# Cross-attention on one Trainium2 core: projection pieces on four 32-column tiles, issued behind PV

## The reference

```python
q = _split_heads(hidden_states @ w_q, HEADS)
k = _split_heads(text @ w_k, HEADS)
v = _split_heads(text @ w_v, HEADS)
out_text = _merge_heads(_sdpa(q, k, v))              # softmax(q k^T / 4) v
out_ip = _merge_heads(_sdpa(q, k_ip, v_ip, mask=mask_ip))
out = (out_text + IP_SCALE * out_ip) @ w_out + b_out + residual
```

## Time and profile before

| | |
|---|---|
| median of 3 runs | 2136.64 us (2120.46 to 2138.08) |
| profiled execution | 2130.14 us, span of the records 2128.3 us |
| TensorE matmul busy | 2011.5 us, 95% of the span |
| VectorE busy | 1341.9 us, 63% |
| ScalarE busy | 1231.1 us, 58% |
| GpSimd busy | 275.6 us, 13% |
| mean granted TensorE clock | 0.978 of full speed |

### The profile page before, as it was taken

The page is one execution under the profiler, slowest core; times in us unless marked ns, Lnnn a source line. Parts: engine busy times, 40 slices in busy tenths (PEclk is TensorE's granted clock), DMA queues, the critical chain, the costliest instruction groups (busy, mean ns, idle before and its releaser), DMA issues.

```text
span 2128.3 us, 31016 instructions
## 1 busy us (share of the span) xinstructions
PE 2011.5 (95%) x12048; PEld 824.6 (39%) x12048; DVE 1341.9 (63%) x1623; ACT 1231.1 (58%) x2364; POOL 275.6 (13%) x314
## 2 busy tenths in 40 slices
PE   4899999997999999999999999999999999999987
PEld 2443334432344333443334433444334443344332
DVE  4757666565665676666755667656766567666660
ACT  0256566555565566555655566655666556665665
POOL 3001111101111011111111111011110111111100
PEclk8999899999999999999999999999999999999999
DMA  7234433353333544435333353333533344443301
GB/s 196 53 53 84 112 67 74 74 117 75 63 76 71 129 81 76 76 66 144 68 70 72 68 141 61 73 61 73 134 66 76 64 119 90 83 77 67 74 21 41
DMA packets 94309, 174.86 MB, mean 82 GB/s; under 512 B 37937, under 2 KB 62386, under 8 KB 90322
## 3 DMA queue, kind: packets, MB, share of 16 engines
q1 hardware_dynamic: 86066, 144.55, 35.1%
q10 hardware_dynamic: 7936, 28.18, 3.9%
q0 software_dynamic: 160, 0.14, 0.1%
HBM read 117.75 MB, written 48.82 MB: 78 GB/s over the span
## 4 chain that ended last, share of the span: by engine, by line
PE 84%; DMA 4%; issue 4%; ACT 4%; DVE 2%; ACTq 1%; SPq 1%; POOL 0%; POOLq 0%
PE pv_bank L580 22%; PE exp_bank L566 19%; PE max_bank L548 14%; PE work_bank L474 10%; PE work_bank L445 10%; PE work_bank L489 3%; PE work_bank L455 3%; DMA q_stack<-neg_rows 3%; ACT probs L754 2%; DVE quarter_max L853 1%; PE work_bank L467 1%; ACT probs_tail L754 1%; ACTq L738 1%; ACTq L763 1%; DMA ctxt<-in_ctx_t 0%
## 5 line engine op out<-in xcount | busy, mean ns | idle before, releaser
L853 DVE TENSOR_REDUCE quarter_max<-max_bank 128x2 f32<-128x800 f32 x1280 | 1232.4, 989 | 692.0 <-PE max_bank L548 687.7
L754 ACT ACTIVATE probs<-exp_bank 128x512 f32<-128x512 f32 x1872 | 1016.2, 595 | 528.3 <-PE exp_bank L566 501.0
L548 PE MATMUL max_bank<-k_stack,q_stack 48*128 48x400 f32 x2560 | 542.7, 384 | 55.9 <-issue 28.2
L566 PE MATMUL exp_bank<-q_stack,k_stack 50*128 50x512 f32 x1872 | 507.3, 469 | 19.9 <-ACT probs L754 19.7
L580 PE MATMUL pv_bank<-probs,v_ones 128*17 128x512 f32 x3840 | 512.5, 606 | 2.0 <-ACT probs L754 2.0
L566 PEld LDWEIGHTS exp_bank<-q_stack,k_stack 50*128 50x128 f32 x1872 | 227.9, 186 | 501.6 <-ACT probs L754 473.5
L548 PEld LDWEIGHTS max_bank<-k_stack,q_stack 48*128 48x128 f32 x2560 | 271.8, 189 | 244.7 <-issue 105.5
L445 PE MATMUL work_bank<-ctxt,wk 128*64 128x400 f32 x1280 | 257.8, 523 | 12.9 <-DMA ctxt<-in_ctx_t 11.1
L474 PE MATMUL work_bank<-wv,ctxt 128*128 128x320 f32 x768 | 246.1, 455 | 0.4 <-ACT neg_rows L698 0.4
L996 POOL TENSOR_TENSOR k_parts<-k_full,zero 128x400 fp32r<-128x400 f32 x80 | 68.2, 852 | 930.4 <-ACT k_full L698 930.4
L474 PEld LDWEIGHTS work_bank<-wv,ctxt 128*128 128x128 f32 x768 | 136.3, 191 | 85.5 <-issue 39.9
(11 more groups left out here) (86 smaller groups left out, 585.4 us busy)
## 6 DMA issues: line engine op xcount, KB each, us to landing
k_stack<-scratch_k SPq DMA_DIRECT2D x240, 200.0 KB, 6.1
scratch_k<-k_parts SPq DMA_DIRECT2D x80, 400.0 KB, 4.7
ctxt<-in_ctx_t ACTq DMA_DIRECT2D x28, 800.0 KB, 9.1
q_stack<-scratch_q SPq DMA_DIRECT2D x240, 64.0 KB, 2.3
scratch_q<-q_parts SPq DMA_DIRECT2D x80, 128.0 KB, 6.7
r_wide<-scratch_r SPq DMA_DIRECT2D x40, 256.0 KB
o_t<-o_sum SPq DMA_DIRECT2D x160, 32.0 KB, 2.0
xres<-in_x SPq DMA_DIRECT2D x8, 640.0 KB, 4.3
```

Source lines behind the costliest of these rows:

```text
L548: last = nc.tensor.matmul(max_bank[:, (u % 2) * 2 + side, 0:CHUNK], exact(q_stack[stack, slot, c, t * 128:(t + 1) * 128]), exact(k_stack[s ...
L566: nc.tensor.matmul(bank[:, :], exact(k_stack[stack, slot, c, kt * 128:(kt + 1) * 128]), exact(q_stack[stack, slot, c, :]), start=True, sto ...
L754: nc.scalar.activation(dst, exp_place(n, final), ACT.Exp, scale=SCALE).then_inc(probs_ready, 1)
L853: nc.vector.reduce_max(quarter_max[:, :, u // QUARTERS, u % QUARTERS], max_bank[:, (u % 2) * 2:(u % 2) * 2 + 2, 0:CHUNK], AX.X).then_inc(m ...
```

## The change

Each projection matmul of K, Q, V, OUT and IP is cut along its output partitions into strips of 32 (`strips`), so that it becomes up to four matmuls with 32 weight columns each, on the four 32-column tiles that PV uses. The moving operand is the same and is read by each strip. K and Q, which were two 64-column matmuls, become four of 32. Q's third contraction tile now has 128 rows instead of 64; the missing rows of `wq` and `xt` are set to zero once (two VectorE memsets, and the waits on `cleared` count two more). WA, WB, TA and TB keep their form. Then, in TensorE's program, `work` moves from the end of the step to directly behind `pv_tile`, ahead of exponent tiles 2 and 3 and of the last units. No other engine's order changes.

```diff
+            def strips(rows):
+                return [(at, min(32, rows - at)) for at in range(0, rows, 32)]
...
-                        last = nc.tensor.matmul(work_bank[half * GR:(half + 1) * GR, 0:CHUNK],
-                                                wk[:, ct, (g % NG) * GR:(g % NG + 1) * GR], ctxt[:, ct, keys:keys + CHUNK],
-                                                start=(ct == 0), stop=(ct == CT - 1))
+                        for at, rows in strips(GR):
+                            dims = (g % NG) * GR + at
+                            last = nc.tensor.matmul(work_bank[half * GR + at:half * GR + at + rows, 0:CHUNK],
+                                                    wk[:, ct, dims:dims + rows], ctxt[:, ct, keys:keys + CHUNK],
+                                                    start=(ct == 0), stop=(ct == CT - 1))
...
-                        last = nc.tensor.matmul(work_bank[:, 0:D], ctxt[:, ct, t * 128:(t + 1) * 128], wv[:, ct, :],
-                                                start=(ct == 0), stop=(ct == CT - 1))
+                        for at, rows in strips(128):
+                            key = t * 128 + at
+                            last = nc.tensor.matmul(work_bank[at:at + rows, 0:D], ctxt[:, ct, key:key + rows], wv[:, ct, :],
+                                                    start=(ct == 0), stop=(ct == CT - 1))
...
                             pv_tile(group_no - 1, (g - 1) % NG, FULL)
+                        if (g, kt) in plan:
+                            work(b, *plan[g, kt], first, last)
                         if kt < FULL:
                             exp_tile(group_no, kt, 2)
                             exp_tile(group_no, kt, 3)
                         next_units(places[2])
-                        if (g, kt) in plan:
-                            work(b, *plan[g, kt], first, last)
...
             nc.vector.memset(zero[:, :], 0.0).then_inc(cleared, 1)
+            nc.vector.memset(wq[64:128, 2, :], 0.0).then_inc(cleared, 1)
+            nc.vector.memset(xt[64:128, 2, :], 0.0).then_inc(cleared, 1)
```

More of the change, by code:

```diff
@@ L452, in q_piece @@
                 for ct in ct_range:
-                    rows = (128, 128, 64)[ct]
                     for half in range(2):
[L455 to L458, removed]
+                        for at, rows in strips(GR):
+                            dims = (g % NG) * GR + at
+                            last = nc.tensor.matmul(work_bank[half * GR + at:half * GR + at + rows, 0:QHALF],
+                                                    wq[:, ct, dims:dims + rows], xt[:, ct, half * QHALF:(half + 1) * QHALF],
+                                                    start=(ct == 0), stop=(ct == 2))
                 if ct_range[-1] == 2:
@@ L466, in ip_piece @@
                 for n in range(2):
-                    last = nc.tensor.matmul(work_bank[:, n * 64:(n + 1) * 64], q_full[:, n * 128:(n + 1) * 128],
-                                            kip_own[:, g % NG, :, :].rearrange("p h t -> p (h t)"), start=True, stop=True)
+                    for at, rows in strips(128):
+                        last = nc.tensor.matmul(work_bank[at:at + rows, n * 64:(n + 1) * 64],
+                                                q_full[:, n * 128 + at:n * 128 + at + rows],
+                                                kip_own[:, g % NG, :, :].rearrange("p h t -> p (h t)"), start=True, stop=True)
                 last.then_inc(work_full, 1)
             def v_piece(t, ct_range):
-                if t < FULL:
-                    for ct in ct_range:
-                        last = nc.tensor.matmul(work_bank[:, 0:D], ctxt[:, ct, t * 128:(t + 1) * 128], wv[:, ct, :],
-                                                start=(ct == 0), stop=(ct == CT - 1))
-                else:
-                    for ct in ct_range:
-                        for odd in range(2):
-                            last = nc.tensor.matmul(work_bank[odd * TAIL:odd * TAIL + TAILV, 0:D],
-                                                    ctxt[:, ct, FULL * 128:TEXT], wv[:, ct, :],
-                                                    start=(ct == 0), stop=(ct == CT - 1))
+                for ct in ct_range:
+                    if t < FULL:
+                        for at, rows in strips(128):
+                            key = t * 128 + at
+                            last = nc.tensor.matmul(work_bank[at:at + rows, 0:D], ctxt[:, ct, key:key + rows], wv[:, ct, :],
+                                                    start=(ct == 0), stop=(ct == CT - 1))
+                    else:
+                        for odd in range(2):
+                            for at, rows in strips(TAILV):
+                                key = FULL * 128 + at
+                                last = nc.tensor.matmul(work_bank[odd * TAIL + at:odd * TAIL + at + rows, 0:D],
+                                                        ctxt[:, ct, key:key + rows], wv[:, ct, :],
+                                                        start=(ct == 0), stop=(ct == CT - 1))
                 if ct_range[-1] == CT - 1:
@@ L487, in out_piece @@
                 for k in k_range:
-                    rows = (128, 128, 97, 128)[k]
-                    last = nc.tensor.matmul(bank, o_t[0:rows, k, t * 128:(t + 1) * 128], wout[0:rows, k, :],
-                                            start=(k == 0), stop=(k == k_end))
+                    deep = (128, 128, 97, 128)[k]
+                    for at, rows in strips(128):
+                        last = nc.tensor.matmul(bank[at:at + rows, :], o_t[0:deep, k, t * 128 + at:t * 128 + at + rows],
+                                                wout[0:deep, k, :], start=(k == 0), stop=(k == k_end))
                 if k_range[-1] == k_end:
@@ L615, in _ @@
                     pe.wait_ge(x_loaded, 32)
+                    pe.wait_ge(cleared, 3)
                     q_piece(piece[1], share(3, turn))
@@ L627, in _ @@
                 else:
-                    pe.wait_ge(cleared, 7)
+                    pe.wait_ge(cleared, 9)
                     negative_piece(0)
@@ L781, in _ @@
                     copy(vip[0:64, 2, :], work_bank[0:64, 128:192]).then_inc(work_empty, 1)
-                    act.wait_ge(cleared, 7)
+                    act.wait_ge(cleared, 9)
                 elif piece[0] == "V":
```

## The result

| | before | changed |
|---|---|---|
| median | 2135.72 us (2120.46 to 2138.08, 4 runs) | 2357.49 us (2341.85 to 2359.82, 4 runs) |
| ratio | | 1.104, 95% interval 1.097 to 1.111 |
| profiled execution | 2130.14 us | 2359.51 us |
| mean granted clock | 0.978 | 0.975 |

The change makes the kernel 10.4% slower. The forecast was 2382 us, 1% above what was measured, in a range of 2320 to 2465.

What follows compares the result with a forecast made beforehand. The prediction took ScalarE's 1.67 us wait, open in every step, as the bound: each step 3.26 us plus W. Net 262 - 6 - 20 - 1 = +235, plus 10 for the clock, gave 2375 profiled, 2382 median, range 2320 to 2465.

Steps and rivals of the forecast that it cites:

- The floor of 3.26 us: Step without a piece: PV 0.98, ScalarE's wait 1.67, tile 1 to PV 0.61; light pieces hide under it.
- W: Streaming time of a piece behind PV: whole V or OUT 2.15 us, halves 1.08, K 1.34 or 0.67, IP 0.4.
- the faster rival: All steps: form changes vanish and nothing waits, near 0.4 us saved a step, about 1955 us; chance 0.03.
- The sum: Over 441 steps, new less old length by kind of piece: 262 us more, net +235 after savings elsewhere.
- the small four: Four small pieces, unchanged in form, priced between nothing and one K tile (0.67): 37 x 0.4 = 15 us.
- 26 saved: At kt = 12, 6 us saved on the switch; at group starts, about 20 of roughly 30 us stack-load waits gone.
- the 6 for the switch: At kt = 12 the order stays and only the change of form goes: 39 x 0.15 = 6 us saved.
- 10 for the clock: Over the whole kernel, 10 us added to the net +235 for TensorE's clock.
- No further cost: Steps with three units: the last waits for VectorE until 1.77 us behind tile 2's load, when tile 1's weights are in.
- The switches go and nothing waits: All steps: a V step takes 4.33 us against 4.70, 176 us saved in all, about 1955 us; chance 0.03.
- Strips don't run together: Pieces: strips reading the same moving data cost 1.3 passes, adding 130 us (2510), or far more one after another; chance 0.03.
- The clock rival: TensorE idles about 0.7 us a step, so its clock falls more often, adding 130 to 150 us, about 2520; chance 0.05.

Runs made afterwards that it cites:

- short exponents: Exponent tiles on ScalarE cut to 64 of 512 columns behind the first group: changed kernel 2230.22 us, ratio 1.045; kernel before 2120.03 us, ratio 0.993.
- short maxima alone: Changed kernel with VectorE's row maxima over 100 of 400 columns, exponents whole: 2310.56 us, ratio 1.081 to the kernel before.

## Why the prediction held, step by step

*What bounds it.* The floor of 3.26 us, read from one step without a piece, and the claim that the light pieces are free under it, carried the forecast. Moving the cover from one side of the exponents to the other makes each step 3.26 and W; seven of the eight kinds agree within 0.01 to 0.02 us. The average, TensorE 95% busy, would have led to the faster rival.

*W.* Streaming at full-width rate was right (0.268 us a round). Only IP was off: its eight matmuls of 64 columns take 3.49 - 3.27 = 0.22 us, where I had 0.40 and 0.3 as the least.

*The sum.* All steps added up from PV start to PV start give +232 us, and the parts outside the steps -3. By kinds, forecast and measured (262 and 235 in all): whole V and OUT 44 and 44, cut in two 67 and 66, K cut in two 50 and 47, K cut in four 40 and 34, whole Q 12 and 11, Q cut in three 19 and 6, IP 15 and 6, the small four 15 and 20. Between the profiled executions the forecast was +245 and the measured +229; the miss of 16 us is mainly in Q and IP. For Q cut in three the step itself was right (3.70); but before there were single long steps among them (one of 4.82 us behind ScalarE's issue of four context loads), which the longer steps shortened (4.07 in the same place), and I had multiplied a clean window by 45. K cut in four has the same fault: seven of its 60 steps wait for VectorE, took 4.84 to 5.09 us before and take 4.85 now, and so paid nothing. At kt = 12 and the group starts I had 26 saved and 19 came; of the 6 for the switch the eight steps with K at the end of the second group gave about 1 (4.61 to 4.46 us each). In the last group of the last batch, which has no pieces and which I left out, 14 us were lost to the clock, where I had put 10 for the clock over the whole. So the steps were 27 us too high, and some 11 of these were made up by what was saved less and by the clock; that the total came within 1% is in part luck. The medians, 2136 and 2357, are 222 apart, the forecast had 246: the kernel before was profiled 6 us under its median, and the changed one 2 above.

*VectorE.* "No further cost" was right, by a narrow margin and for the changed kernel alone. As the short exponents showed, it was a second bound 0.1 us under the first; with the exponents cut it kept 0.6 us in the steps with two units in a row. Where VectorE comes late from IP, it sets the step both before the change and after it.

*The rivals.* "The switches go and nothing waits" is wrong in its second half. The switches do go: a V step at the new place is 5.615 us in the old form and 5.41 in strips. The Trainium skill, "TensorEngine Tiling (Array Packing)", Key Properties, says that changing the mode drains TensorE; the 0.20 us between these two kernels, first weights included, agree. "Strips don't run together" is excluded by the rounds of 0.268, one full-width pass each. The 3.07x that the prediction took from the Trainium skill, "TensorE: Matmul & The Clock Gate", Part 3, is the page's figure for four row tiles; strips are column tiles. The clock rival decided nothing over the whole (0.975 against 0.978) but does show at single places, as the last section has it.

## What to carry to other kernels

Before work is moved next to its like to save a switch, look at what it covers where it stands: here two waits for ScalarE had one cover each. In a whole V step joining the covers saved about 0.4 us, by the prediction's estimate (0.20 of it measured, at the joint with PV), and the step became 0.71 longer, so that about 1.1 were opened; a step with a light piece became longer by the whole of the piece. The price can be read beforehand from a step that has nothing in the slot. When a wait is shortened, work out which comes next; here VectorE's lay 0.1 us under ScalarE's, and behind both the stack loads at the group starts.

## What was not expected of the hardware

In the last group of the last batch, where the program of before and after is the same but for its entrance, the changed kernel ran at the lower of the clock's two levels, 1.2 instead of 2.4 GHz:

```profile
2264.00:2281.00 17.00, 15.39 (x83) 5.56 (x75) 11.03 (x13) 9.35 (x18) 1.03 (x1) 0.81 0.04 9
2281.00:2305.00 24.00, 20.45 (x98) 5.94 (x98) 4.33 (x8) 15.19 (x30) 1.28 (x1) 0.78 0.04 13
2305.00:2346.00 41.00, 35.60 (x211) 9.27 (x211) 0.25 (x1) 18.80 (x36) 0.70 (x1) 0.62 0.09 27
```

The figures with a count in brackets are the busy us of the five engines; the one behind them is PEclk, the granted clock. By the clock records it is at the lower level from 2253 to 2270 us, at the full one until 2294, and at the lower one again for 41 us, that is for the whole group. A step of this group then takes 3.32 us instead of 2.16, and the group 41.6 instead of 27.5. In the 40 us ahead of the second fall TensorE paused for 0.3 to 0.7 us at a time and once, at the group start, for 1.8. The kernel before and the one with short maxima alone have the same pause of 1.8 us at this place, and both ran the group at the full clock; the old pieces at the new place have it too and ran the group at 3.32 us a step. So the pauses alone don't decide it, and what does stays open. It need not be so in every execution either: over its four runs the changed kernel had a mean clock of 0.975 to 0.987, and the one with 0.987 was the fastest, 2341.85 us.
